# Row maxima of two heads by a pair of 64-row matmuls, read by one VectorE instruction

## What is computed

```
x_n = group_norm(x)                       # 32 groups
q, k, v = conv1x1(x_n, wq|wk|wv) + bias   # to (b, 4 heads, 1024, 64)
attn = softmax(q @ k.T * 64 ** -0.5)
out  = conv1x1(attn @ v, wp) + bp
return x + out
```

## Time and profile before

| | |
|---|---|
| median of 3 runs | 374.97 us |
| span of the profiled execution | 373.5 us |
| what the runs have beside that span | about 1.5 us |
| TensorE matmuls, busy | 358.6 us, 4581 instructions |
| VectorE, busy | 309.5 us |
| ScalarE, busy | 311.7 us |
| GpSimd, busy | 257.9 us |
| granted TensorE clock | full in all 40 slices |

### The profile page before, as it was taken

How to read it: one execution, slowest core, us unless ns; L and a number is a source line. 1 busy time by engine, 2 the same in 40 slices (tenths; PEclk the granted TensorE clock), 3 DMA queues, 4 the chain that set the end, 5 groups by cost and what they waited for, 6 DMA issues and landing times.

```text
span 373.5 us, 11249 instructions
## 1 busy us (share of the span) xinstructions
PE 358.6 (96%) x4581; PEld 227.6 (61%) x4581; DVE 309.5 (83%) x569; ACT 311.7 (83%) x393; POOL 257.9 (69%) x227
## 2 busy tenths in 40 slices
PE   1999999999999999999999999999999999999996
PEld 1734575656566665756666566656657666665674
DVE  4799888889978788889988788888888888899784
ACT  1758799989778999988887999988878888889883
POOL 5045887778496887949667796958758495757722
PEclk9999999999999999999999999999999999999999
DMA  6045250252532530342633430022542432050113
GB/s 215 17 129 148 44 123 9 30 156 57 110 116 63 116 100 2 83 132 46 136 121 73 93 92 30 17 72 44 126 146 45 89 84 73 2 182 19 31 32 112
DMA packets 38731, 30.92 MB, mean 83 GB/s; under 512 B 23820, under 2 KB 31512, under 8 KB 38680
## 3 DMA queue, kind: packets, MB, share of 16 engines
q1 hardware_dynamic: 37936, 29.15, 31.4%
q10 hardware_dynamic: 744, 1.06, 0.8%
HBM read 9.44 MB, written 4.19 MB: 37 GB/s over the span
## 4 chain that ended last, share of the span: by engine, by line
PE 76%; SPq 9%; DVE 4%; ACT 4%; DMA 3%; issue 2%; DVEq 1%; ACTq 0%
PE gen L524 16%; PE st L604 12%; PE st L605 12%; PE mx L583 11%; PE pv L627 7%; PE pv L630 7%; PE pv L629 7%; DMA q_max<-shift 3%; SPq L415 2%; SPq L394 2%; DVE mx L884 2%; PE st L524 1%; ACT st L808 1%; ACT p_hi L801 1%; DVE p_lo L905 1%
## 5 line engine op out<-in xcount | busy, mean ns | idle before, releaser
L884 DVE TENSOR_REDUCE mx<-mx 128x1 f32<-128x512 f32 x256 | 173.4, 687 | 31.5 <-PE mx L583 25.5
L801 ACT ACTIVATE p_hi<-st 128x1024 f16<-128x1024 f32 x127 | 130.3, 1026 | 39.2 <-PE st L605 38.2
L1128 POOL TENSOR_TENSOR p_lo<-p,p_hi 128x1024 f16<-128x1024 f32 x62 | 132.1, 2132 | 32.6 <-ACT p L808 32.5
L627 PE MATMUL pv<-v_hi,p_hi 128*128 128x65 f16 x1024 | 105.7, 194 | 0.5 <-DVE o L913 0.5
L630 PE MATMUL pv<-v_hi,p_lo 128*128 128x65 f16 x1024 | 105.9, 194 | 0.0
L629 PE MATMUL pv<-v_lo,p_hi 128*128 128x64 f16 x1024 | 105.7, 193 | 0.0
L627 PEld LDWEIGHTS pv<-v_hi,p_hi 128*128 128x128 f16 x1024 | 94.5, 98 | 12.9 <-DVE o L913 2.5
L629 PEld LDWEIGHTS pv<-v_lo,p_hi 128*128 128x128 f16 x1024 | 93.6, 98 | 14.1
L604 PE MATMUL st<-q_twice,k_both 128*128 128x512 f16 x256 | 97.2, 380 | 1.6 <-DMA q_max<-shift 0.9
L605 PE MATMUL st<-q_max,k_one 65*128 65x512 f16 x256 | 97.3, 380 | 0.0
L630 PEld LDWEIGHTS pv<-v_hi,p_lo 128*128 128x128 f16 x1024 | 93.7, 97 | 0.0
(11 more groups left out here) (173 smaller groups left out, 466.5 us busy)
## 6 DMA issues: line engine op xcount, KB each, us to landing
q_twice<-st_hi_q SPq DMA_DIRECT2D x64, 64.0 KB, 2.1
xres<-in_x_dram SPq DMA_DIRECT2D x4, 1024.0 KB, 5.4
out_dram<-y SPq DMA_DIRECT2D x13, 256.0 KB, 2.8
xin<-in_x_dram SPq DMA_DIRECT2D x6, 512.0 KB, 4.4
k_both<-st_hi_k SPq DMA_DIRECT2D x16, 128.0 KB, 2.3
k_one<-st_hi_k SPq DMA_DIRECT2D x16, 128.0 KB, 2.4
q_max<-st_lo_q SPq DMA_DIRECT2D x32, 64.0 KB, 2.1
k_both<-st_lo_k SPq DMA_DIRECT2D x16, 128.0 KB, 2.3
```

Of the source, the lines that this page charges most:

```text
L627: nc.tensor.matmul(pv_v[:, q, :], hi, vh, start=k == 0 and q == 0, stop=False, skip_group_check=True)
L801: nc.scalar.activation(p_hi[:, G % PR, :, :], scores, ACT.Exp, scale=SM_SCALE / M_SCALE)
L884: nc.vector.reduce_max(mx8[:, U % 2, tile, part:part + 1], mxb[j % 2][:, :], AX.X)\
L1128: nc.gpsimd.tensor_tensor(p_lo[:, G % PR, :, :], p_full(G), p_hi[:, G % PR, :, :], ALU.subtract)\
```

## The change

From the third unit pair on, the maxima of two heads with the same queries' half are made together. A *pair item* ("two", V, m) is two matmuls with a contraction of 64 rows: head 0 of the pair in rows 0 to 63 of the array into bank 0, head 1 in rows 64 to 127 into bank 1. V counts unit pairs (units 2V and 2V + 1), m the 8 combinations of query tile and key half. Pairs for V = 3 to 15 stand one a slot from 10 slots ahead (`PAIR_AHEAD`); V = 2 has a table of slots 8 to 13. Units 0 to 3 keep single maxima. Only the high keys take part in a pair: the product with the low keys is left out of the estimate.

The two banks become one tile of two banks, reduced by one VectorE instruction over 2 x 512 columns. A pair waits until all earlier reductions are done. Joining, shift (ScalarE) and shift row are once per V, with two transfers. For the first half of the queries a pair reads `kq_hi` directly; GpSimd therefore waits, before it overwrites `kq_hi`, for the pairs that read it. In `k_both` the high keys of head 1 now stand in rows 64 to 127. On TensorE the first maximum now stands right after the scores, ahead of a job's second half.

```diff
+    SINGLES = 4
+    PAIR_AHEAD = 10
+    FIRST_PAIRS = {8: (0,), 9: (1,), 10: (2, 3), 11: (4,), 12: (5, 6), 13: (7,)}
...
-        mxb = [pb("mx0"), pb("mx1")]
+        mx = pb("mx", 2)
+        mxb = [mx[:, 0:512], mx[:, 512:1024]]
...
+        def single_maxima(G):
+
+            U, n = divmod(G + MX_AHEAD, SPU)
+            return [("one", U, 2 * n), ("one", U, 2 * n + 1)] if U < SINGLES else []
+
+        def pair_maxima(G):
+
+            V, m = divmod(G + PAIR_AHEAD, 2 * SPU)
+            if G in FIRST_PAIRS:
+                return [("two", SINGLES // 2, m) for m in FIRST_PAIRS[G]]
+            return [("two", V, m)] if SINGLES // 2 < V < B * UNITS // 2 else []
+
         def maxima_at(G):
+            return single_maxima(G) + pair_maxima(G)
...
             def shift_to_row(U):
                 _, head, half = unit(U)
-                wait(sp, s_shift, U + 1)
-                sp.dma_start(q_max[D:D + 1, head, halves(half)], shift[:, U % 2, :]).then_inc(s_shift_dma, 16)
+                wait(sp, s_shift, joined(U))
+                for h in units_joined(U):
+                    sp.dma_start(q_max[D:D + 1, head - U % 2 + h, halves(half)], shift[:, U // 2 % 2, h, :])\
+                      .then_inc(s_shift_dma, 16)
...
+            def pair_of_maxima(V, m):
+
+                b, head, half = unit(2 * V)
+                tile, part = pair_part(m)
+                if half == 0:
+                    wait_hi(pe, "q", nth(head // 2, 0, b) + 1)
+                    wait_hi(pe, "k", nth(head // 2, part, b) + 1)
+                elif m == 0:
+                    wait(pe, s_dup_k, 16 * 6 * (V // 2 + 1))
+                    wait(pe, s_dup_q[1], 16 * 6 * (V // 2 + 1))
+                wait(pe, s_mx_free, place_of["two", V, m])
+                for h in range(2):
+                    rows = slice(h * D, (h + 1) * D)
+                    if half == 0:
+                        queries, keys = kq_hi["q"][rows, tile_of(0, tile)], kq_hi["k"][rows, halves(part)]
+                    else:
+                        queries = q_twice[rows, head + h, tile_of(1, tile)]
+                        keys = k_both[rows, head + h, halves(part)]
+                    last = nc.tensor.matmul(mxb[h], queries, keys, start=True, stop=True)
+                last.then_inc(s_mx_full, 1)
...
                 if s == 0:
-                    wait(pe, s_shift_dma, 16 * (U + 1))
+                    wait(pe, s_shift_dma, 16 * rows_in(U))
...
             def slot(G):
                 if G < TOTAL:
                     scores(G)
-                top, olds = maxima_at(G), weighed_at(G)
+                tops, olds = maxima_at(G), weighed_at(G)
+                for item in tops[:1]:
+                    maximum(item)
                 begun = job_at(G - 1) if G % 2 else None
                 if begun and begun[0] in LONG:
                     job(*begun, only=1)
-                if top:
-                    maximum(U, n)
                 for old in olds:
                     weigh(old)
...
-                if top:
-                    maximum(U, n + 1)
+                for item in tops[1:]:
+                    maximum(item)
...
+                    nc.vector.reduce_max(mx8[:, n % 2, :, tile, part], mx[:, :].rearrange("p (h k) -> p h k", h=2),
+                                         AX.X).then_inc(s_mx_free, 1)
...
+                elif (i, b) > (0, 0):
+                    gone = 2 * (2 * b + i - 1)
+                    if kind == "k":
+                        wait(pool, s_mx_full, place_of["two", gone, (j + 1) * QT - 1] + 1)
+                    elif j == 0:
+                        wait(pool, s_mx_full, all_full("two", gone))
```

More of the change, by code:

```diff
@@ L419, in slot @@
                 b, g = place(G)
-                U = shift_at(G)
-                if U is not None:
+                for U in complete_at(G - 1):
                     shift_to_row(U)
@@ L580, in maximum @@
                 _, head, half = unit(U)
-                wait(pe, s_mx_free, MXJ * U + j - 1)
+                if j == 0 and U == 2:
+                    pe.wait_ge(s_first_top, 16 * 2)
+                elif j == 0:
+                    wait(pe, s_dup_k, 16 * 6)
+                    wait(pe, s_dup_q[1], 16 * 6)
+                n = place_of["one", U, j]
+                wait(pe, s_mx_free, n - (in_order[n - 1][0] == "one"))
                 tile, part = mx_part(U, j)
-                nc.tensor.matmul(mxb[j % 2][:, :], q_twice[:, head, tile_of(half, tile)], k_both[:, head, halves(part)],
+                nc.tensor.matmul(mxb[j % 2], q_twice[:, head, tile_of(half, tile)], k_both[:, head, halves(part)],
                                  start=True, stop=True).then_inc(s_mx_full, 1)
+            def pair_of_maxima(V, m):
[9 more added lines that the diff above has]
+                for h in range(2):
+                    rows = slice(h * D, (h + 1) * D)
+                    if half == 0:
[5 more added lines that the diff above has]
+                last.then_inc(s_mx_full, 1)
+            def maximum(item):
+                (single_maximum if item[0] == "one" else pair_of_maxima)(*item[1:])
             def scores(G):
@@ L690, in first_maximum @@
                 wait(pe, s_mx_free, MXJ * U + j - 1)
-                nc.tensor.matmul(mxb[j % 2][:, :], kq_hi["q"][rows, tile_of(0, j % QT)], kq_hi["k"][rows, half],
+                nc.tensor.matmul(mxb[j % 2], kq_hi["q"][rows, tile_of(0, j % QT)], kq_hi["k"][rows, half],
                                  start=True, stop=True).then_inc(s_mx_full, 1)
@@ L784, in row_shift @@
             def row_shift(U):
[L786 to L789, removed]
+                wait(act, s_join, joined(U))
+                if U >= SINGLES:
+                    wait(act, s_shift_dma, 16 * rows_in(U - 3))
+                heads = slice(units_joined(U)[0], units_joined(U)[-1] + 1)
+                nc.scalar.activation(shift[:, U // 2 % 2, heads, :], mx4[:, U // 2 % 2, heads, :], ACT.Identity,
+                                     bias=p_log[:, 0:1], scale=-1.0 / M_SCALE).then_inc(s_shift, 1)
             def exponent(G):
@@ L801, in exponent @@
                 nc.scalar.activation(p_hi[:, G % PR, :, :], scores, ACT.Exp, scale=SM_SCALE / M_SCALE)
-                if G > 0 and maxima_at(G - 1) and maxima_at(G - 1)[1] == MXJ - 2:
-                    row_shift(maxima_at(G - 1)[0])
+                if G > 0:
+                    for U in complete_at(G - 1):
+                        row_shift(U)
                 if G == 2 * PB - 1:
@@ L879, in then, with row_max @@
                 dve.drain()
[L881 to L885, removed]
-            def join_max(U):
-                wait(dve, s_mx_free, MXJ * (U + 1))
-                wait(dve, s_shift, U - 1)
-                nc.vector.reduce_max(mx4[:, U % 2, :], mx8[:, U % 2, :, :], AX.X).then_inc(s_join, 1)
+            def row_max(kind, n, j):
+                wait(dve, s_mx_full, place_of[kind, n, j] + 1)
+                if kind == "one":
+                    tile, part = mx_part(n, j)
+                    nc.vector.reduce_max(mx8[:, n // 2 % 2, n % 2, tile, part:part + 1], mxb[j % 2], AX.X)\
+                      .then_inc(s_mx_free, 1)
+                else:
+                    tile, part = pair_part(j)
+                    nc.vector.reduce_max(mx8[:, n % 2, :, tile, part], mx[:, :].rearrange("p (h k) -> p h k", h=2),
+                                         AX.X).then_inc(s_mx_free, 1)
+            def join_max(U):
+                wait(dve, s_mx_free, all_full(*(("one", U) if U < SINGLES else ("two", U // 2))))
+                if U >= SINGLES:
+                    wait(dve, s_shift, joined(U - 3))
+                heads = slice(units_joined(U)[0], units_joined(U)[-1] + 1)
+                nc.vector.reduce_max(mx4[:, U // 2 % 2, heads, :], mx8[:, U // 2 % 2, heads, :, :], AX.X)\
+                  .then_inc(s_join, 1)
             def low(kind, i, j, b):
@@ L964, in slot @@
                     p_low(G - 1)
-                if top:
-                    row_max(U, n)
+                for item in tops[:1]:
+                    row_max(*item)
                 if stat_at(G):
@@ L975, in slot @@
                     channel_stats(b + 2, (g - 20) // 4, ((g - 20) // 2 % 2,))
[L976 to L979, removed]
+                for item in tops[1:]:
+                    row_max(*item)
+                for U in complete_at(G):
+                    join_max(U)
                 if G in (1, 2):
@@ L1055, in _ @@
             for j in range(MXJ):
-                row_max(0, j)
+                row_max("one", 0, j)
             join_max(0)
```

59 lines of the change are left out of this document (35 added, 24 removed).

## The result

| | before | changed |
|---|---|---|
| median, us | 375.01 (374.83 to 375.57, 4 runs) | 385.13 (384.50 to 385.81, 4 runs) |
| ratio to before | | 1.027, 95% interval 1.0254 to 1.0286 |
| span of the profiled execution | 373.5 | 382.8 |

What follows compares the result with a forecast made beforehand. TensorE's matmul rate was taken to bound slots 17 to 111. Early slots +5.5, steady slots +1.1, slots 112 to 117 +1.2, slots 118 to 121 0, shift rows -0.5: +7.3 on 373.5, so 382 us; range 375.5 to 389.

Steps and rivals of the forecast that it cites:

- Steady slot: Slots 17 to 111: a pair's overlap is eaten by two height changes; 0.44 us per pair, +1.1 us for 95 pairs.
- The 4 ns: The Trainium skill's distance between tiles' starts; by it the 95 steady pairs would come to -2.3 us.
- no overlap: Rival: a pair's second matmul starts 0.24 us after the first; +0.21 a slot, 403 us; chance 10%.
- height is free in steady slots: Rival: the 0.09 us per height change is not paid in steady slots; -0.17 a slot, 365 us; chance 10%.
- VectorE keeps up: Steady slots: the pair's reduction, about 1.22 us, stays hidden with 0.8 us of slack, so its wait costs nothing.
- Early slots: Slots 8 to 13: pairs wait for reductions, slot 14 starts 5.9 us late; slots 14 to 16 recover; term +5.5 us.
- Slots 112 to 117: Last image after its projections: six slots take 14.0 us against 12.81; term +1.2 us (0 to +1.5).
- The ring of reductions: Each pair waits for the previous pair's whole reduction, so two slots need 4.7 us in slots 112 to 117.
- The shift rows: Made once in eight slots: three waits go, 1.1 us; second transfers land 0.6 later; term -0.5, slots 118 to 121 0.
- The sum: Whole kernel: all terms together add +7.3 us to the 373.5 us span, giving 380.8 and a time of 382.
- The 1.5 us around the span: Time outside the profiled span, 374.97 less 373.5, taken as unchanged and added to the forecast span.
- The range: Whole kernel: 375.5 to 389 us, said to leave out the two rivals and take the bounds of the terms.

Runs made afterwards that it cites:

- e4: The changed kernel with every pair issued twice in a row, same operands and banks; 403.16 us, steady slot 2.91.
- e10: The kernel before, with the maxima of units 2 to 31 as 64-row matmuls, each alone; 424.02 us, steady slot 3.14.
- e1: The changed kernel with both matmuls of every pair in array rows 0 to 63; 412.89 us, steady slot 2.91.
- run 413: Not a run's number but the whole time of e1, the changed kernel with both matmuls of every pair in rows 0 to 63; measured 412.89 us.
- e7: The changed kernel with only two of the eight early pairs of V = 2; 377.15 us, ratio to before 1.0052.
- e5: The changed kernel with a semaphore for each head's shift transfer, scores waiting for their own head's alone; 380.29 us, ratio to before 1.0125.
- e6: The changed kernel with the two transposing transfers of an output piece one slot later in the queue; 384.28 us, ratio to before 1.0243.
- e2: The changed kernel with both matmuls of every pair over all 128 rows; 387.74 us, steady slot 2.683.

## Why the prediction was right, and where it was off

- **Steady slot: right.** Forecast +0.01 us a slot from overlap less two changes of height; measured +0.011. The mechanism is the one that was forecast, but that the number agrees to 0.001 is luck, as two parts were off and cancel: the second matmul starts 3 ns and not 0.04 us after the first, and going out costs 0.12 and not 0.09, so in and out is 0.22 (e4, e10) and not 0.18. The 4 ns that the prediction set beside its own 0.04 were right; the saving of 2.3 us that it worked out from them did not come, because of the dearer way out. The rival "no overlap" is excluded by e1 (slot 2.91, run 413), the rival "height is free in steady slots" by e10 and by the fence of slot 57.
- **VectorE keeps up: right.** The pair's reduction is 1.22 us as worked out, and steady slots do not wait for it: the eight waits, 3.1 us, are all in slots 10 to 14 and 114. Four steady slots, 34, 36, 66 and 68, take 0.06 to 0.15 more, where ScalarE is late by 0.3 to 0.8.
- **Early slots: right**, +6.1 and -0.5 against +5.9 and -0.5; e7, with two of the eight pairs, takes 5.5 of it away.
- **Slots 112 to 117: too dear.** Forecast +1.2, measured +0.2. The ring of reductions needs its 4.6 us once (slots 114 and 115); the first two slots take 4.11, which fits with the slack that the steady ones leave, and the last two take 4.32, which was not explained.
- **The shift rows: the step that was mis-sized.** I had -0.5 us for slots up to 111 and 0 for the end; measured are +1.5 us (2.5 less the 1.0 of the steady slots; slots 34, 36, 66 and 68 have 0.4 of it) and +1.3. The gains came, and a little larger: slots 27, 59 and 91 are 1.4 us shorter together, against 1.1. The losses were put at 0.6 us, for a second transfer that lands 1.9 us after its issue and finds one place without slack; the five waits cost 3.0 us, since in these five places it landed 3.05 to 3.29 us after its issue, each time beside an instruction packet. The 3.3 stood in the earlier trace rows as the longest landing; the prediction took the 1.9 for all. At the end, the wait is 2.1 us. Of that, 0.9 is for the second head's row, as e5 takes it away; the rest is for the first head's, issued 0.7 us after the start of slot 119, and slots 118 and 120 take 1.6 us, not the 1.95 that was put down for ScalarE. In the profiled execution 0.8 more went to the lower clock in slot 121. e5 takes 4.8 us away.
- **The sum**: +7.3 forecast on the span, +9.3 measured; 382 against 385.1 by the medians. The 1.5 us around the span came from setting a profiled span beside the median of other executions. Beside its own span an execution has about 2.0 us in both kernels (384.76 over 382.8 in the changed one; 375.5 over 373.5 in one of the kernel before that ran beside e5). By this estimate the profiled execution of the kernel before took some 0.5 more than its median, and that of the changed kernel took 0.4 less; that is the 0.8 by which the medians differ more than the spans. The range, 375.5 to 389, does not follow from the bounds of the terms as the prediction says: its own sum of the lower ones is 374.

## What to carry to other kernels

Two matmuls side by side in row halves are worth it only if several stand together: here the visit cost 0.22 us and each pair after the first 0.21, so one pair between 128-row matmuls is no better than two full matmuls in series. Before a change that trades matmuls, look in the trace for one place where the new form already stands beside the old and read the starts on either side. And when one signal comes to cover two transfers, everything that can delay either now delays the wait: a signal for each gave back 4.8 of 10 us.

## What was not expected of the hardware

- Of a 128-packet transfer, 8 packets ended 0.8 us later than the rest; they started as a 16 KB instruction packet ended that had run for 1.1 us.
- After 2.1 us without matmuls in the changed kernel, the clock stayed full for 1.6 us and was then granted 0.53 in the 3.6 us from 357.30 on. In e6 TensorE waited 2.0 us at the same place and the clock stayed full. In e1 the clock fell at 58.3 us, where no wait of the early slots had been longer than 0.9 us, and stayed at 0.50 for 23.9 us in which TensorE had work throughout.
- Two 64-row matmuls of 512 columns in different row halves start 3 ns apart and take 0.41 us together, one takes 0.40; in one half, 0.62.
- Where the height changes, in either direction, the weight load starts 4 to 5 ns ahead of its matmul; in e2, with 128 rows throughout, the same matmuls have it 0.22 us ahead, under the matmul before. Matmuls of 65 and 128 rows follow each other at 0.22, without a pause.
